# A selective-scan layer and its feed-forward block: four decay banks and two dense banks instead of three and three, other chains at both ends, another order

## The chip, the core and the metric

The kernel runs on one core of one Trainium2 chip. A core has five engines with instruction queues of their own: TensorE (PE in the profile; its weight loads are PEld), VectorE (DVE), ScalarE (ACT), GpSimd (POOL) and SyncE (SP), which here only issues transfers. They work side by side and wait for each other through semaphores. The metric is the device time of one execution in microseconds, here the median of several runs.

## What is computed

An input of 8 batches x 512 steps x 128 channels goes through a selective-scan block with 256 inner channels and 16 states, a layer norm, a feed-forward block of 384 hidden units and a second layer norm.

```python
h = x * rsqrt(mean(x * x, -1) + 1e-05) * norm_w
xs, res = split(h @ in_proj_w.T, 2)
u = silu(causal_conv(xs, conv_w, 4 taps) + conv_b)
delta, Bm, Cm = split(u @ x_proj_w.T, [64, 80])
delta = softplus(delta @ dt_proj_w.T + dt_proj_b)
state = exp(delta * A) * state + (delta * u) * Bm        # per channel, state and step
y = (sum_n state * Cm + u * D) * silu(res)
x = layernorm(x + y @ out_proj_w.T + x)
gate, up = x @ wg.T, x @ wu.T                            # weights are int32 / 127
x = layernorm(x + (silu(gate) * up) @ wd.T)
```

## The kernel before

**Layout.** One batch of 512 steps is one iteration k (`Iteration(k)`); the loop runs from k = -1 (set-up and head: only inputs are prepared) to k = 8 (the tail: only outputs are finished). In between one iteration does three things at once: it scans batch k, prepares the inputs of batch k + 1 (`it.ins`) and finishes the outputs of batch k - 1 (`it.outs`).

**The scan.** The 256 x 16 pairs of channel and state are cut into 32 groups of 128 rows (32 channels x 4 states). A group n is one step. ACT makes its decay exp(delta * A) (`exp_decay`, L573) into one of three PSUM banks, `decay_ps[n % DECAYS]`; VectorE runs the recurrence over 512 time steps in one instruction (`scan`, L964); its input is a product du * B that POOL makes for four groups at once (`multiply`, L791, 128 x 2048). Four groups are a quad. After the first scan of the next quad VectorE weighs the four states with C (`weigh`, L973), and TensorE gathers the states into `y_ps` (`sum_states`, "S" in the plan, L441 to L443: at the start of each half with a skip product u * D). C is spread into the bank `c_ps` by TensorE (`spread_c`, "C" in the plan, L432); `weigh(q)` waits for it.

**The dense work.** All other products of TensorE are jobs by name: h (transpose of the scaled input), xs0, xs1 (the convolution, four products each), res0, res1, xd, z0, z1, b0 to b3 (B spread over rows), proj, x1 (transpose), gate0 to gate2, up0 to up2, down. A job writes one of the dense banks (`BANK`), `wait_free` waits until what lay there was taken, and the taker (ACT or VectorE) frees it. delta and du are replicated over rows by transfers on SP's queue (L340).

**Order.** Nothing is scheduled by a program: `PLAN` lists what TensorE does in each of the 8 quads, `ACT_AT` and `DVE_AT` say after which of the 32 scans ACT and VectorE do each dense step, `POOL_AT` after which quad's product POOL does its small steps. On ACT step n stands behind the decay n + 1. Each engine works strictly through its list, so a step that waits holds up all behind it.

**Both ends.** In the head the weights are transposed on TensorE, the taps scaled on VectorE (L881) while POOL builds `pick0` (L744, L752), and softplus of both halves is done before the first decay. In the tail the output of the last batch goes: combination, proj, copy to r1 (L626), statistics (L1005, L984), four POOL steps (L811 to L816), normalisation on ACT (L579), x1, the gates, down, copy to y_out (L675), and the same norm again.

The names that the prediction uses: `combine` (L980), `gate` (L989), `gate_up` (L995), `take_b` (L610), `soften_first` (L912 to L941), `multiply_first` (L950).

Of the kernel before, what the change touches and what calls it, by code (L numbers as in the profile page):

```python
# [20 lines left out]
def mamba_swiglu_postln(nc, x, norm_w, in_w, conv_w, conv_b, xp_w, dt_w, dt_b, a_log, d_skip, out_w,  # L21
# [28 lines left out]
    with ctx:  # L50
# [1018 lines left out]
```

## Time and profile before

| | us |
|---|---|
| median of 3 runs (590.15 to 590.64) | 590.59 |
| the profiled execution | 589.53 |
| its span, first to last instruction | 587.8 |
| VectorE busy in it | 514.7 (88%) |
| TensorE busy | 420.6 (72%) |
| POOL busy | 418.9 (71%) |
| ACT busy | 368.8 (63%) |
| mean granted TensorE clock | 0.81 |

A row of a timeline has the start in us from the span's first instruction, the duration in us, the engine, the line, the operation, what it writes and reads, and a count where neighbours are merged; in brackets stands the idle time of the engine before it and what ended it. Neighbours on an engine overlap by some 0.08 us, so a step costs a little less than its duration. PEclk 1.00 is TensorE at 2.4 GHz, 0.50 at 1.2 GHz. A float32 product of 512 columns runs as two passes, so it counts as x2.

### The profile page before, as it was taken

Reading aid. Unit: us, or ns where it says so; the run is one execution under the profiler, and the core shown is the slowest. Engines: PE = TensorE matmul, PEld = TensorE weight load, DVE = VectorE, ACT = ScalarE, POOL = GpSimd, SP = SyncE. Lnnn points to the kernel's source line nnn. Section 1 sums busy time; section 2 is a strip of 40 time slices with the busy share of each in tenths; the row PEclk is TensorE's granted clock in tenths of the full one; section 3 lists DMA queues with packets and bytes.
Section 4 is the critical chain, followed back from the end, with each engine's and each line's share of the span. In section 5 each row is a group of like instructions: output and inputs, shape, how many; then the busy total and the mean of one; then the engine's idle time right before and its main releaser. Section 6 shows DMA issues by size and latency. Waiting matters only on the chain. (4 is left out here: it accounts for less than half of the span.)

```text
span 587.8 us, 5583 instructions
## 1 busy us (share of the span) xinstructions
PE 420.6 (72%) x1509; PEld 183.4 (31%) x1509; DVE 514.7 (88%) x552; ACT 368.8 (63%) x587; POOL 418.9 (71%) x219
## 2 busy tenths in 40 slices
PE   2977644996769766978779776977699674477653
PEld 2422111421424214422433233422442142224322
DVE  5788689988999899988999899989998899999622
ACT  2493965489557965598458956597549954553031
POOL 7559499767895789767986698577975799583111
PEclk9978856797869797897869787998879786757767
DMA  7051424600651043401460063202350065100000
GB/s 215 8 130 38 120 39 104 144 0 0 144 119 42 1 96 82 109 18 24 120 144 20 0 141 87 76 0 66 78 141 18 0 143 131 32 1 0 1 18 18
DMA packets 27366, 39.18 MB, mean 67 GB/s; under 512 B 3816, under 2 KB 10056, under 8 KB 27344
## 3 DMA queue, kind: packets, MB, share of 16 engines
q1 hardware_dynamic: 25424, 38.51, 27.6%
q10 hardware_dynamic: 1920, 0.42, 0.4%
q8 instruction: 9, 0.15, 0.1%
q14 instruction: 13, 0.11, 0.1%
HBM read 3.27 MB, written 2.10 MB: 9 GB/s over the span
## 5 line engine op out<-in xcount | busy, mean ns | idle before, releaser
L791 POOL TENSOR_TENSOR prod<-du_rep,b_rep 128x2048 f32<-128x2048 f32 x63 | 286.1, 4543 | 57.4 <-DVE state L964 49.7
L964 DVE TENSOR_TENSOR_SCAN state<-decay_ps,prod 128x512 f32<-128x512 f32 x256 | 300.3, 1208 | 22.0 <-ACT decay_ps L573 14.6
L573 ACT ACTIVATE decay_ps<-delta_rep,a_neg 128x512 f32<-128x512 f32 x252 | 170.8, 689 | 111.0 <-DVE state L964 110.5
L973 DVE TENSOR_TENSOR weighted<-state,c_ps 128x2048 f32<-128x2048 f32 x64 | 145.1, 2267 | 4.8 <-PE c_ps L432 4.2
L443 PE MATMUL y_ps<-weighted,gather 128*32 128x512 f32 x512 | 85.2, 745 | 37.7 <-DVE weighted L973 37.7
L463 PE MATMUL dense_ps<-h_t,tap_t 128*128 128x512 f32 x128 | 71.0, 706 | 0.4 <-ACT h_t L621 0.4
L432 PE MATMUL c_ps<-bc,pick 64*128 64x512 f32 x64 | 37.6, 588 | 44.8 <-DVE weighted L973 44.8
L811 POOL TENSOR_TENSOR ve<-mv,epsm 128x4 f32<-128x4 f32 x16 | 3.3, 203 | 66.5 <-DVE mv L984 66.4
L463 PEld LDWEIGHTS dense_ps<-h_t,tap_t 128*128 128x128 f32 x128 | 28.0, 230 | 48.0 <-issue 47.0
L432 PEld LDWEIGHTS c_ps<-bc,pick 64*128 64x128 f32 x64 | 13.7, 215 | 93.2 <-DVE weighted L973 60.7
L495 PE MATMUL dense_ps<-x_t,up_t 128*128 128x512 f32 x48 | 32.5, 766 | 9.2 <-DVE g_act L989 9.2
L495 PE MATMUL dense_ps<-x_t,gate_t 128*128 128x512 f32 x48 | 34.7, 812 | 4.9 <-DVE g_act L995 4.1
L500 PE MATMUL dense_ps<-down_t,g_act 128*128 128x128 f32 x192 | 37.1, 346 | 1.4 <-DVE g_act L995 1.4
L443 PEld LDWEIGHTS y_ps<-weighted,gather 128*32 128x32 f32 x512 | 10.9, 117 | 76.6 <-DVE weighted L973 45.8
L500 PEld LDWEIGHTS dense_ps<-down_t,g_act 128*128 128x128 f32 x192 | 33.4, 256 | 4.5 <-issue 4.5
L989 DVE SCALAR_TENSOR_TENSOR g_act<-g_th,dense_ps 128x512 f32<-128x512 f32 x24 | 16.4, 684 | 14.6 <-ACT g_th L666 14.6
L799 POOL TENSOR_TENSOR z_ln<-z_ln,z_pos 128x512 f32<-128x512 f32 x15 | 19.3, 1286 | 13.0 <-ACT z_ln L659 13.0
L610 ACT ACTIVATE b_rep<-dense_ps 128x512 f32<-128x512 f32 x30 | 16.1, 590 | 16.7 <-PE dense_ps L478 16.7
L456 PE MATMUL dense_ps<-ident,hx 128*128 128x128 f32 x32 | 8.3, 412 | 25.2 <-ACT hx L587 25.2
L795 POOL TENSOR_TENSOR z_wm<-z_e,z_wm 128x512 f32<-128x512 f32 x15 | 18.7, 1270 | 9.9 <-ACT z_wm L650 6.4
L483 PE MATMUL dense_ps<-out_t,g 128*128 128x128 f32 x128 | 22.6, 305 | 2.3 <-DVE g L980 2.3
L626 ACT ACTIVATE r<-dense_ps 128x512 f32<-128x512 f32 x8 | 4.8, 597 | 28.8 <-PE dense_ps L487 28.8
(130 smaller groups left out, 607.8 us busy)
## 6 DMA issues: line engine op xcount, KB each, us to landing
du_rep<-z_wm SPq DMA_DIRECT2D x64, 256.0 KB, 4.6
delta_rep<-z_ln SPq DMA_DIRECT2D x64, 256.0 KB, 4.5
out_dram<-y_out SPq DMA_DIRECT2D x8, 256.0 KB, 2.2
state<-L_attn_in_proj_w_in ACTq DMA_DIRECT2D x1, 256.0 KB, 4.1
x_all<-L_attn_x_in SPq DMA_DIRECT2D x1, 256.0 KB, 4.5
weighted<-L_ffn_w_gate_in SPq DMA_DIRECT2D x1, 192.0 KB, 10.6
weighted<-L_ffn_w_up_in SPq DMA_DIRECT2D x1, 192.0 KB, 3.3
weighted<-L_ffn_w_down_in SPq DMA_DIRECT2D x1, 192.0 KB, 4.4
```

Of the source, the lines that this page charges most:

```text
L432: mm(c_ps[:, :], pick[R:, CHUNKS + quad % CHUNKS, :], bc[it.now][R:, :], start=True, stop=True).then_inc(c_ready, 1)
L443: last = mm(y_ps[DB * c:DB * c + DB, :], gather[:, :], weighted[quad % 2][:, c, :], start=False, stop=(q == CHUNKS - 1), tile_position=(0, ...
L463: last = mm(ps[:, :], tap_t[:, n, j, :], h_t[:, j:j + T], start=(j == 0), stop=(j == TAPS - 1))
L483: mm(ps[:, i * P:(i + 1) * P], g[:, h, i * P:(i + 1) * P], out_t[:, h, :], start=(h == 0), stop=False)
L495: last = mm(ps[:, :], (gate_t if kind == "gate" else up_t)[:, n, :], x1_t[:, :], start=True, stop=True)
L500: mm(ps[:, i * P:(i + 1) * P], g_act[:, b, i * P:(i + 1) * P], down_t[:, b, :], start=(b == 0), stop=False)
L573: A(decay_ps[n % DECAYS][:, :], decay_ps[n % DECAYS][:, :] if spread_first else delta_rep[:, h, c, :], ACT.Exp, scale=a_neg[:, col:col + 1 ...
L791: TT(prod[quad % 2][:, :, :], du_rep[:, h, :, :], b, ALU.mult).then_inc(prod_ready, 1)
L795: TT(z_wm[:, h, :], z_e[:, h, :], z_wm[:, h, :], ALU.subtract).then_inc(soft_step, 1)
L799: TT(z_ln[:, h, :], z_ln[:, h, :], z_pos[:, h, :], ALU.add).then_inc(soft_step, 1)
L964: dve.tensor_tensor_scan(state[n // BLOCKS % 2][:, n % BLOCKS, :], decay_ps[n % DECAYS][:, :], prod[n // BLOCKS % 2][:, n % BLOCKS, :], 0. ...
L973: TT(weighted[quad % 2][:, :, :], state[quad % 2][:, :, :], c_ps[:, :].unsqueeze(1).broadcast_to([P, BLOCKS, T]), ALU.mult).then_inc(weigh ...
```

## The change

`DECAYS` is 4, so `DENSE` is 2: four PSUM banks for decays and two for dense jobs. `PLAN`, `BANK`, `ACT_AT`, `DVE_AT` and `POOL_AT` are new. The functions `stir` and the tables `STIR_HEAD`, `STIR_TAIL` are there, but all their counts are 0 and the plan names no such product, so nothing is issued by them.

```diff
-    DECAYS = 3
+    DECAYS = 4
     DENSE = 6 - DECAYS
@@
-                ["up1", "gate2", "up2", "C", "S", "b0", "b1"],
-                ["C", "b2", "b3", "down", "S"],
+                ["up0", "gate1", "C", "up1", "S", "gate2"],
+                ["b0", "b1", "up2", "C", "down", "b2", "b3", "S"],
@@
-        DVE_AT = {"combine": (22, 3), "stats1": 9, "gate": (20, 21, 23), "up": (21, 23, 24), "stats2": 29}
+        DVE_AT = {"combine": (18, 3), "stats1": 7, "gate": (19, 20, 23), "up": (20, 21, 25), "stats2": 29}
+        STIR_HEAD = {"h": 0, "xs0": 0, "du0": 0}
+        STIR_TAIL = {"S": 0, "x1": 0, "gate0": 0}
```

In `ACT_AT` the steps move so: y 9 to 4, h 1 to 0, silu 11 to 10, xd and x1n 13 to 15, z 15 and 16 to 16 and 17, z's exponential, z_w and z_wm 16, 17, 18 to 17, x1 16 to 17, ln 20 to 19, gates 19, 21, 24 to 18, 19, 24, b 24, 24, 29, 29 to 25, 26, 28, 28, down 29 to 27.

**TensorE around quad 4 and 5.** Here are C (L432), the gates and ups (L495), the skip product (L441) and the gathers (L443), of a middle batch. Before:

```order
L495 MATMUL dense_ps1<-x1_t,gate_t 128x512
L495 MATMUL dense_ps2<-x1_t,up_t 128x512
L495 MATMUL dense_ps0<-x1_t,gate_t 128x512
L495 MATMUL dense_ps1<-x1_t,up_t 128x512
L495 MATMUL dense_ps2<-x1_t,gate_t 128x512
L495 MATMUL dense_ps0<-x1_t,up_t 128x512
L432 MATMUL c_ps<-bc1,pick 128x512
L441 MATMUL y_ps<-u_1,skip_t 128x512
L443 MATMUL y_ps<-weighted0,gather 32x512 x4
```

After (C is L442, gates and ups L526, skip L454, gathers L456):

```order
L526 MATMUL dense_ps1<-x1_t,gate_t 128x512
L526 MATMUL dense_ps0<-x1_t,up_t 128x512
L526 MATMUL dense_ps1<-x1_t,gate_t 128x512
L442 MATMUL c_ps<-bc1,pick 128x512
L526 MATMUL dense_ps0<-x1_t,up_t 128x512
L454 MATMUL y_ps<-u_1,skip_t 128x512
L456 MATMUL y_ps<-weighted0,gather 32x512 x4
L526 MATMUL dense_ps1<-x1_t,gate_t 128x512
```

The ups and the last gate have moved behind C and behind the gathers, and gate1 and gate2 stand in one bank.

**TensorE around quad 6.** b0 to b3 are `bc,pick` (L478 before, L497 after), down is `down_t,g_act`. Before:

```order
L478 MATMUL dense_ps1<-bc0,pick 128x512
L478 MATMUL dense_ps2<-bc0,pick 128x512
L432 MATMUL c_ps<-bc1,pick 128x512
L478 MATMUL dense_ps2<-bc0,pick 128x512
L478 MATMUL dense_ps0<-bc0,pick 128x512
L500 MATMUL dense_ps1<-down_t,g_act 128x128 x3
L502 MATMUL dense_ps1<-x1,ident 128x128
```

After:

```order
L497 MATMUL dense_ps1<-bc0,pick 128x512
L497 MATMUL dense_ps0<-bc0,pick 128x512
L526 MATMUL dense_ps1<-x1_t,up_t 128x512
L442 MATMUL c_ps<-bc1,pick 128x512
L529 MATMUL dense_ps0<-x1,ident 128x128 x4
L533 MATMUL dense_ps0<-down_t,g_act 128x128 x12
L497 MATMUL dense_ps0<-bc0,pick 128x512
L497 MATMUL dense_ps1<-bc0,pick 128x512
L456 MATMUL y_ps<-weighted1,gather 32x512 x4
```

b2 and b3 have moved behind down, and up2 stands behind b0.

**TensorE at the start of a batch.** h is `ident,hx`, xs0 is `h_t,tap_t`. Before:

```order
L456 MATMUL dense_ps1<-ident,hx 128x128 x4
L432 MATMUL c_ps<-bc0,pick 128x512
L443 MATMUL y_ps<-weighted1,gather 32x512 x4
L463 MATMUL dense_ps1<-h_t,tap_t 128x512 x4
L465 MATMUL dense_ps2<-h_t,res_t 128x512
L483 MATMUL dense_ps0<-out_t,g 128x128 x2
```

After:

```order
L475 MATMUL dense_ps0<-ident,hx 128x128 x4
L482 MATMUL dense_ps1<-h_t,tap_t 128x512 x4
L456 MATMUL y_ps<-weighted1,gather 32x512 x4
L442 MATMUL c_ps<-bc0,pick 128x512
L502 MATMUL dense_ps0<-x_all,twice 128x128 x4
L506 MATMUL dense_ps0<-out_t,g 128x128 x8
```

xs0 has moved ahead of the gathers and of C; in the projection the products with x (`twice`) stand ahead of those with g.

**proj and down.** Both now add x first and then wait for g or for the last up product:

```diff
                 elif kind == "proj":
+                    for i in range(TILES):
+                        ...
+                        mm(ps[:, i * P:(i + 1) * P], twice[:, :], xk, start=(i == 0), stop=False)
                     it.wait(pe, g_ready, HALVES, -1, HALVES)
@@
                 elif kind == "down":
+                    for i in range(TILES):
+                        mm(ps[:, i * P:(i + 1) * P], ident[:, :], x1[:, i, :], start=(i == 0), stop=False)
                     it.wait_taken(pe, f"up{HID - 1}")
```

**The head.** Its jobs have an order and banks of their own; the first two products of du and B are made on VectorE from TensorE's spread du; z1's softplus and the weights of the feed-forward block move into batch 0; POOL's second select waits for the scaled taps; ACT loads the exp table ahead of xd.

```diff
-        HEAD_JOBS = ["h", "xs0", "xs1", "res0", "xd", "res1", "z0", "z1", "b1", "b0", "b2", "b3"]
+        HEAD_JOBS = ["h", "xs0", "res0", "xs1", "res1", "xd", "z0", "z1", "b0", "du0", "du1", "b1", "b2", "b3"]
@@
-                        for c in range(BLOCKS):
+                        for c in (2, 3, 0, 1):
                             replicate(du_rep, du, 0, c, du_in)
@@
+                elif kind == "du":
+                    pe.wait_ge(du_ready, 1)
+                    last = mm(ps[:, :], spread[:, n, :], du[:, 0, :], start=True, stop=True)
+                elif kind == "gate" and it.k0 == 0:
+                    pe.wait_ge(ffn_float, 3)
+                    raw = (gate_f[:, :, :], up_f[:, :, :], down_f.rearrange("p (b h) -> p b h", b=HID))[n]
+                    for b in range(HID):
+                        last = turn(ps[:, b * P:(b + 1) * P], raw[:, b, :], ident[:, :])
@@
+                silu(it, name, dst, h)
+                A(a_neg[:, 0:1], cw[:, 0, 0:1], ACT.Exp)
                 take_xd(it)
@@
+                    if it.k0 == 0:
+                        head_it = Iteration(-1)
+                        if n == 0:
+                            second_half(head_it)
+                        if n == 1:
+                            for q in (1, 2, 3):
+                                take_b(head_it, q)
+                        if n == 3:
+                            late_copy()
                     dense(it, n)
+                    if it.k0 == 0 and n == 2:
+                        second_log()
@@
             TT(x_rs[:, 0:TILES], x_ms[:, 0:TILES], powm[:, 0:TILES], ALU.pow).then_inc(rs_ready, 1)
+            pool.wait_ge(in_scaled, HALVES)
             sel(out=pick0, in_=pick0, compare_op=ALU.not_equal, fill=1.0, base=-XC,
@@
             def error(it, h):
                 it.wait(pool, wm_ready, 1, 1, 1)
                 TT(z_wm[:, h, :], z_e[:, h, :], z_wm[:, h, :], ALU.subtract).then_inc(soft_step, 1)
+                it.wait(pool, soft_step, 4, 1, 2 * h + 1)
+                TT(z_wm[:, h, :], z_wm[:, h, :], z_pos[:, h, :], ALU.add).then_inc(soft_step, 1)
```

**The tail.** In iteration 8 the copies to r1 and y_out and ACT's normalisation are left out; VectorE takes the statistics from PSUM and normalises by itself, POOL only takes the power:

```diff
+            def last_scale(ve, ve_ready, rs, rs_ready_):
+                pool.wait_ge(ve_ready, 1)
+                TT(rs[:, :], ve[:, :], powm[:, 0:TILES], ALU.pow).then_inc(rs_ready_, 1)
@@
+            def last_norm(it, name, st, step, mv, mv_ready, ve, ve_ready, rs, rs_ready_, dst, done):
+                it.wait_full(dve, name)
+                src = it.ps(name)[:, :].rearrange("p (i m) -> p i m", m=M)
+                for i in range(TILES):
+                    last = dve.bn_stats(st[:, i, :], src[:, i, :])
+                ...
+                TS(ve[:, :], mv[:, :, 1], EPS, None, ALU.add).then_inc(ve_ready, 1)
+                dve.wait_ge(rs_ready_, B)
+                for i in range(TILES):
+                    last = TS(dst[:, i, :], src[:, i, :], mv[:, i, 0:1], rs[:, i:i + 1], ALU.subtract, ALU.mult)
+                last.then_inc(done, 1)
```

## Rows read from the trace of the kernel before

**Rows 1.** Windows, first to last scan: length, busy PE, PEld, DVE, ACT, POOL, PEclk, DMA
```profile
38.66:549.51 510.85, 377.14 (x1362) 159.35 (x1360) 479.41 (x487) 340.53 (x541) 390.51 (x183) 0.81 0.29 68
```

**Rows 2.** Timeline of VectorE: start, duration (us), line, operation, idle before
```profile
166.00 1.19 DVE L964 TENSOR_TENSOR_SCAN state<-decay_ps,prod 128x512 f32<-128x512 f32 x1
...
489.60 1.19 DVE L964 TENSOR_TENSOR_SCAN state<-decay_ps,prod 128x512 f32<-128x512 f32 x1
...
496.25 0.67 DVE L980 TENSOR_TENSOR g<-y_ps,sres 128x512 f32<-128x512 f32 x1
...
497.96 2.26 DVE L973 TENSOR_TENSOR weighted<-state,c_ps 128x2048 f32<-128x2048 f32 x1
500.14 4.56 DVE L964 TENSOR_TENSOR_SCAN state<-decay_ps,prod 128x512 f32<-128x512 f32 x4
...
549.70 2.25 DVE L973 TENSOR_TENSOR weighted<-state,c_ps 128x2048 f32<-128x2048 f32 x1
```

**Rows 3.** Waits of VectorE in one batch, 230.62 to 295.24: total, times, longest
```profile
DVE state L964 <- ACT decay_ps L573: 2.3, 3, 1.6
DVE g_act L989 <- ACT g_th L666: 0.8, 1, 0.8
```

**Rows 4.** Windows, four stretches at one granted clock each (PEclk)
```profile
62.90:66.10 3.20, 3.20 (x4) 0.88 (x3) 3.20 (x2) 2.66 (x4) 0.00 (x0) 0.50 0.91 222
...
219.90:223.10 3.20, 3.20 (x14) 2.78 (x14) 3.20 (x4) 1.45 (x3) 3.12 (x3) 0.50 0.84 216
...
230.20:240.30 10.10, 7.38 (x18) 2.81 (x19) 10.10 (x13) 6.50 (x12) 9.45 (x7) 0.50 0.75 174
240.40:264.10 23.70, 20.00 (x82) 8.37 (x80) 21.52 (x24) 18.75 (x32) 14.80 (x8) 1.00 0.10 27
```

**Rows 5.** Timeline of TensorE, batch 0 and a middle batch
```profile
61.21 1.13 PE L465 MATMUL dense_ps<-h_t,res_t 128*128 128x512 f32 x2 [2.68 <-ACT u L592]
...
181.29 1.13 PE L441 MATMUL y_ps<-u,skip_t 128*128 128x512 f32 x2
...
183.35 3.70 PE L463 MATMUL dense_ps<-h_t,tap_t 128*128 128x512 f32 x8
...
200.06 1.94 PE L443 MATMUL y_ps<-weighted,gather 128*32 128x512 f32 x8 [3.18 <-DVE weighted L973]
201.93 0.79 PE L432 MATMUL c_ps<-bc,pick 64*128 64x512 f32 x1
...
204.52 1.85 PE L495 MATMUL dense_ps<-x_t,up_t 128*128 128x512 f32 x2
...
208.39 1.13 PE L495 MATMUL dense_ps<-x_t,up_t 128*128 128x512 f32 x2 [1.17 <-DVE g_act L989]
...
219.09 0.50 PE L432 MATMUL c_ps<-bc,pick 64*128 64x512 f32 x1 [2.93 <-DVE weighted L973]
...
220.32 1.65 PE L500 MATMUL dense_ps<-down_t,g_act 128*128 128x128 f32 x6
...
223.58 0.83 PE L500 MATMUL dense_ps<-down_t,g_act 128*128 128x128 f32 x6
```

**Rows 6.** Groups of the page, POOL's product
```profile
L791 POOL TENSOR_TENSOR prod<-du_rep,b_rep 128x2048 f32<-128x2048 f32 x63 | 286.1, 4543 | 57.4 <-DVE state L964 49.7
```

**Rows 7.** Head: the scalings (min, median, max ns), POOL's select, a table load
```profile
L881 DVE TENSOR_SCALAR delta_rep<-state,cw x8: 279/282/3529, 7.0 to 11.0; 128x128 f32<-128x128 f32 x8
...
8.14 3.01 POOL L752 TENSOR_SCALAR_AFFINE_SELECT delta_rep<-delta_rep 128x1024 f32<-128x1024 f32 x1
...
27.51 1.28 ACT L696 ACT_TABLE_LOAD   x1
```

**Rows 8.** Chain that ended last, three pieces of the tail: start us, us, what
```profile
559.18 0.61 ACT r L626
...
562.93 1.66 ACT x L579 x4
...
566.59 6.93 PE dense_ps L495 x10
```

More of the change, by code:

```diff
@@ new lines, in mamba_swiglu_postln @@
+        BANK = {"h": 0, "xs0": 1, "proj": 0, "xs1": 0, "res0": 1, "res1": 0, "xd": 1, "z0": 0, "z1": 1, "x1": 0,
+                "gate0": 1, "up0": 0, "gate1": 1, "up1": 0, "gate2": 1, "up2": 1, "b0": 1, "b1": 0, "down": 0,
+                "b2": 0, "b3": 1}
+        ACT_AT = {"hx": 0, "y": 4, "h": 0, "r1": 7, "silu": 10, "xd": 15, "x1n": 15, "z": (16, 17), "x1": 17,
+                  "ze": 17, "zw": 17, "zwm": 17, "ln": 19, "gate": (18, 19, 24), "b": (25, 26, 28, 28), "down": 27}
+        DVE_AT = {"combine": (18, 3), "stats1": 7, "gate": (19, 20, 23), "up": (20, 21, 25), "stats2": 29}
@@ L275, in __init__ @@
                 self.names = jobs_of(k0)
-                earlier = [n for k in range(-1, k0) for n in jobs_of(k)]
-                self.before = [sum(BANK[n] == b for n in earlier) for b in range(DENSE)]
+                earlier = [bank_of(k, n) for k in range(-1, k0) for n in jobs_of(k)]
+                self.before = [earlier.count(b) for b in range(DENSE)]
             def count(self, each, batch, n):
@@ L387, in _ @@
             pe.wait_ge(ident_ready, 1)
+            for _ in range(STIR_HEAD["h"]):
+                mm(c_ps[:, 0:P], ident[:, :], ident[:, :], start=True, stop=True)
             for h in range(HALVES):
@@ L507, in iteration @@
                     for name in it.names:
+                        if name == "h":
+                            early_weights()
                         if name == "xs0":
-                            early_weights()
+                            for _ in range(STIR_HEAD["xs0"]):
+                                stir(it, name)
                             pe.wait_ge(wt_taken, 1)
@@ L535, in iteration @@
                         if name == "C":
-                            if it.scan:
+                            if it.scan and not (it.k0 == 0 and quad == 0):
                                 spread_c(it, quad)
@@ L659, in dense @@
                     A(z_ln[:, :, :], z_e[:, :, :], ACT.Ln, bias=1.0).then_inc(ln_ready, 1)
+                if it.k0 == 0:
+                    for b in range(HID):
+                        if step == at["gate"][b]:
+                            name = f"gate{b}"
+                            it.wait_full(act, name)
+                            it.take(A((gate_t, up_t, down_t)[b][:, :, :].rearrange("p b h -> p (b h)"),
+                                      it.ps(name)[:, 0:HID * P], ACT.Copy, scale=(1.0, 1.0, SILU2)[b]), name)
                 if it.outs:
```

296 lines of the change are left out of this document (163 added, 133 removed).

## The prediction

> **What bounds the kernel now.** I read the stretches first. Between the first scan and the last, 38.66 to 549.51 us, VectorE is busy 479.41 of 510.85 us [rows 1]; ahead of it lie 38.7 us of set-up, behind it 38.3 us of tail. Then I read VectorE's own timeline, to see how far it is from its own pace. Batch 7, which prepares no successor, never waits: its first scan starts at 489.60 and its last weighing (L973) at 549.70, so 60.1 us is what a batch costs VectorE alone. The batches before it take (489.60 - 166.00) / 5 = 64.7 us [rows 2]. So 4.6 us a batch are waits. The waits of one batch name ACT's decays (2.3 us) and the tanh (0.8) [rows 3]; the remainder is the overlap lost around them. What could be won in the middle is thus 6 batches x 4.6 = 28 us, no more.
>
> Last I read TensorE. It has two speeds: it is granted 1.00 in 240.4 to 264.1 us and 0.50 (1.2 instead of 2.4 GHz) in 230.2 to 240.3 [rows 4]. It fell after it had idled 3.18 us (the eight gathers from 200.06 took 1.94), 2.93 us (the stretch from 219.9 to 223.1) and, in batch 0, 2.68 us, where it was at 0.50 from 62.9 us; it did not fall after 1.17 us [rows 4, 5]. Once low it stayed so for 3.2 to 10 us, while it worked nearly without a pause. At 0.50 two passes of a 512-column product take 1.85 us instead of 1.13, or 1.0 in a stream; the next value of C 0.79 instead of 0.50; three down products of 128 columns 1.65 instead of 0.83 [rows 5].
>
> **The change, part by part.** *Four decay banks.* ACT may run four scans ahead instead of three, one scan (1.12 us, 4.48 for four [rows 2]) more. That covers the longest ACT wait before, 1.6 us, only together with the moved steps, and ACT's own work does not shrink: in steps 15 to 19 it now has xd, x1, both z, three 1,024-wide steps and the logarithm in a row. I take these ACT waits as gone, -2.3 us, which is part of the 4.6 and is not counted twice: I build the new batch from 60.1 up.
>
> *Two dense banks and the new order.* Nothing is added or removed on VectorE. What counts is each place where VectorE now meets a chain over TensorE.
>
> Place 1, the third gate. From the end of quad 4's weighing VectorE has three products (0.67 less 0.08 of overlap) and three scans until it wants tanh(gate2): 3 x 0.59 + 3 x 1.12 = 5.1 us. In that time TensorE must do C, up1, the skip product with four gathers, and gate2, one behind the other since the bank of gate2 is that of gate1: 0.50 + 1.13 + 2.06 (181.29 to 183.35) + 1.13, and ACT a tanh of 0.59: 5.4 us less the overlaps, so no slack at full clock. At half clock it is 0.79 + 1.85 + 3.9 + 1.85 + 0.59 = 9.0, 3.9 us late [rows 2, 5]. Before, all gates and ups stood ahead of C. Just before this place TensorE waits for the weighing: gate1 ends about 2.2 us ahead of it. I take a fall, and a climb back halfway: 2.0 us late; ends 0 and 3.9.
>
> Place 2, the down projection. b2 and b3 now stand behind it. From the last up product (step 25) to the next batch's first scan VectorE has six scans, one weighing and the statistics: 6.7 + 2.2 + 1.0 = 9.9 us. The chain in that time: twelve down products (4 x 0.68), the copy 0.6, b2 and b3 on TensorE and, behind a decay, on ACT (0.8 + 1.3), and POOL's product of 4.54 [rows 6]: 9.9. Again no slack, and the decay of step 29 waits behind the copy too. TensorE has 3 us of idle in the 4.7 ahead of it (tanh, b0's copy, the weighing). At half clock each group of three costs 1.44 instead of 0.68 before its neighbour starts: 3.0 us late in all. I take 1.9; ends 0 and 3.0. Before, b2 and b3 stood ahead of down, and POOL's product did not wait for it.
>
> Place 3, the batch's start. xs0 now stands ahead of the gathers and C. VectorE wants the gathers 1.12 + 2.18 + 3 x 1.12 = 6.7 us after its first scan starts. TensorE starts xs0 about 0.6 to 1.1 after it (it waits for hx, a transpose and the copy of h, some 2 to 3 us with little work in it): 3.70 + 1.1 makes 5.4 to 5.9, in time; at half clock 0.6 + 7.3 + 1.9 = 9.8, 3.1 late [rows 5]. I take 1.5.
>
> Place 4, z1. ACT needs it in step 17, ahead of three steps of 1 us each and the decay of step 19. TensorE idles 2.35 us until xd is copied, then does z0, C, the gathers and z1, 3.4 us, with 1 us to spare; at half clock 6.2, so 1.8 late. I take 0.8. Place 5, gate0 behind x1's copy: ends 0 and 1.9, I take 0.3, since place 4 has spread the work.
>
> The sum is 2.0 + 1.9 + 1.5 + 0.8 + 0.3 = 6.5, a batch of 66.6 us, 1.9 above the present one: 6 batches make +11.4. Batch 7 has places 1 and 5 and an idler TensorE, against nothing before: I take +3.0 (ends 0 and 5).
>
> The idle stretches that the new order leaves are 2.0 to 2.7 us (2.7 between x1 and the gathers of quad 3), between the row of 1.17 that kept the clock and that of 2.68 that lost it, and often two lie close together; they are nearer to 2.68, so I price them as falls.
>
> The Trainium skill (TensorE: Matmul & The Clock Gate, Why this matters for your kernels) advises to leave no idle gaps of more than about 3 us between bursts. By that rule no gap of the new order would cost the clock. The rows above hold two falls after less, 2.93 and 2.68 us, so the rule is not safe here; what it would make is the first rival.
>
> *The head.* POOL's second select on pick0 now waits for VectorE's scaling of the taps. Before, one of the eight scalings took 3.53 us instead of 0.28, beside that select of 3.01 [rows 7]; free of it they are done 3.2 earlier. The res products stand between xs0, xs1 and xd: +1.9 less overlap, and the transposes ahead of h: together +2.0. An exp table load of 1.28 [rows 7] goes under the xd products, an addition of 0.7 leaves the chain behind the logarithm, z1's part (three steps of 0.65 and two loads, 4.5 us) moves behind the first decays, and the first two products come from TensorE instead of a DMA, but VectorE waits for them: -1.3, -0.7, -4.5 and +1.7. The first scan moves from 38.7 to about 32.7. But the moved part stands again between decays 1 and 4: scan 4 gains about 2.3 us, and POOL's products, two of which VectorE waits for in batch 0, leave 2.0 at its end. I take -2.0; ends -6 and +1.
>
> *The tail.* Gone: the copy of r1 (0.61), that of y_out (0.6), two short POOL steps each time (about 0.4), part of each ACT normalisation (1.66 against four VectorE instructions of about 0.28) [rows 8], the x products behind g and behind the last up product (1.3 and 0.9). Added: gate2 and up2 share a bank, so the FFN piece of 6.93 plus its activations becomes about 1.6 longer. Sum -4.2; ends -6 and 0, the worse if TensorE stays low throughout.
>
> Total: 11.4 + 3.0 - 2.0 - 4.2 = +8.2 on the profiled execution's 589.5 us: 597.7. The median of the runs is 1.1 above that execution: 598.8, so 599 us.
>
> **Rivals.** *Full clock in spite of the gaps.* If gaps under 2.7 us cost nothing, every place above has its slack of about zero and a batch takes 60.3 us: 6 x -4.4 - 2.0 - 4.2 = -32.6, so 558 us. For it: the row of 1.17, and that TensorE stays at 1.00 for 23.7 us in the middle of each batch. Against: 2.68 and 2.93.
>
> *Falls at half of the places.* Faster, with one mechanism: the clock falls only after the longest gap, between x1 and the gathers, and ahead of place 1, and is back before down. It decides at place 2: while POOL's product is in time the batch keeps 1.9 us, and place 3 another 1.3. A batch of 63.4: 6 x -1.3 + 2.0 - 2.0 - 4.2 = -12, so 579 us. For it: in the present batches the low stretches end after 3.2 to 7 us in two cases of three.
>
> *An exchange.* The waits add up to the old 4.6 and only the ends differ: 6 x 0 + 2 - 6.2 = -4, to 0 with a poorer tail: 587 to 591.
>
> *Worse.* TensorE stays at 0.50 through most of the batch, since it never works long enough at a stretch: stalls of 8.4, a batch of 68.5: 6 x 3.8 + 4 - 6 = +21, 611 us.
>
> **The numbers.** The forecast has a chance of 0.48 (its own range 592 to 606), worse 0.09, exchange 0.12, half of the places 0.19, full clock 0.12. A measurement of this kernel tells about 0.2%, 1.2 us, from no change. Faster takes full clock, half and most of the exchange: 0.37; same 0.06; slower 0.57. The range runs from 570, which leaves full clock out, to 609.
>
> **What would show it.** Right: first scans of batches 66 to 67 us apart; VectorE waiting in each batch about 2 us for the tanh of gate2, about 2 us for POOL's first product and 1 to 2 us ahead of the combination in step 3 for TensorE's gathers; hardly any wait for decays outside step 19; the eight scalings done by 8.7 us; the first scan near 33 us; a tail of about 34 us. Wrong: a granted clock of 1.00 through the batch, a spacing under 62, or scans waiting mainly for ACT, which would mean that the fourth bank and not TensorE decides.

## The result, and the profile after

The changed kernel is slower: 599.85 us in the median (598.34 to 603.11, 4 runs) against 590.62 for the kernel before (590.15 to 591.46, 4 runs), a ratio of 1.016 with a 95% interval of 1.012 to 1.021. The forecast was 599, with a range of its own from 592 to 606. The profiled execution took 603.11 us (span 601.4), the longest of the four, so sizes read from it are some 3 us too large in sum; most of these may sit in the head (see the last section).

| stretch (us, from the profiles) | before | after | difference | forecast |
|---|---|---|---|---|
| start to first scan | 38.66 | 37.15 | -1.5 | -6.0 |
| batch 0 | 62.95 | 66.75 | +3.8 | +4.0 |
| batches 1 to 6, each | 64.67 | 66.71 | +2.04 (x6: +12.3) | +1.9 (+11.4) |
| batch 7, first to last scan | 58.71 | 61.96 | +3.25 | +3.0 |
| last scan to end | 39.44 | 35.24 | -4.2 | -4.2 |
| span | 587.8 | 601.4 | +13.6 | +8.2 |

(The forecast put -2.0 on the first two rows together: 6.0 won ahead of the first scan, 4.0 lost again in batch 0.)

From the start of the first scan to the end of the last, as in [rows 1]: length, busy PE, PEld, DVE, ACT, POOL, PEclk, DMA.

```profile
37.15:567.33 530.18, 399.63 (x1376) 163.37 (x1374) 479.95 (x489) 347.45 (x549) 390.97 (x184) 0.80 0.28 66
```

VectorE is busy as long as before (479.95 against 479.41), in 19.3 us more. So all of the loss between the scans is idle time of VectorE. Its waits over batches 1 to 6, with the one ahead of batch 7's first scan (total, times, longest):

```profile
DVE g_act L1079 <- ACT g_th L720: 13.2, 16, 2.2
DVE state L1038 <- ACT decay_ps L620: 8.8, 9, 1.5
DVE state L1038 <- POOL prod L864: 7.6, 6, 1.4
DVE g L1054 <- PE y_ps L456: 4.4, 3, 1.8
DVE g_act L1085 <- PE dense_ps L526: 0.6, 2, 0.4
```

These are 34.6 us, 5.8 a batch, against 3.6 before by the same count. Of the 3.6, [rows 3] has 2.3 for decays and 0.8 for the tanh; the same view has a third wait, for C ahead of a weighing, which the prediction took for lost overlap:

```profile
DVE weighted L973 <- PE c_ps L432: 0.5, 1, 0.5
```

Here is batch 5 on VectorE (371.09 to 438.14, 67.05 us), the instructions that wait and the next first scan; in brackets the idle time and who ended it:

```profile
371.09 1.22 DVE L1038 TENSOR_TENSOR_SCAN state<-decay_ps,prod 128x512 f32<-128x512 f32 x1 [1.21 <-POOL prod L864]
...
408.61 0.69 DVE L1079 SCALAR_TENSOR_TENSOR g_act<-g_th,dense_ps 128x512 f32<-128x512 f32 x1 [1.02 <-ACT g_th L720]
...
419.73 0.69 DVE L1079 SCALAR_TENSOR_TENSOR g_act<-g_th,dense_ps 128x512 f32<-128x512 f32 x1 [1.31 <-ACT g_th L720]
...
432.43 1.22 DVE L1038 TENSOR_TENSOR_SCAN state<-decay_ps,prod 128x512 f32<-128x512 f32 x1 [1.45 <-ACT decay_ps L620]
...
438.14 1.23 DVE L1038 TENSOR_TENSOR_SCAN state<-decay_ps,prod 128x512 f32<-128x512 f32 x1 [1.21 <-POOL prod L864]
```

The first and the last row are POOL's first product, for this batch and for the next; between them stand gate0, gate2, and the decay of step 29 behind the copy of y_out. These are places 5, 1 and 2 of the prediction. TensorE in the same batch, at the places where its clock fell:

```profile
396.10 0.95 PE L493 MATMUL dense_ps<-xd,dt_t 64*128 64x512 f32 x1 [2.41 <-ACT xd L652]
...
403.28 1.94 PE L456 MATMUL y_ps<-weighted,gather 128*32 128x512 f32 x8 [1.85 <-DVE weighted L1047]
...
405.87 2.07 PE L526 MATMUL dense_ps<-x_t,gate_t 128*128 128x512 f32 x2
...
412.74 0.50 PE L442 MATMUL c_ps<-bc,pick 64*128 64x512 f32 x1 [1.96 <-DVE weighted L1047]
413.33 2.02 PE L526 MATMUL dense_ps<-x_t,up_t 128*128 128x512 f32 x2
...
423.79 0.79 PE L442 MATMUL c_ps<-bc,pick 64*128 64x512 f32 x1 [1.00 <-DVE weighted L1047]
```

And the granted clock (the last number but two) of those stretches:

```profile
396.50:399.50 3.00, 3.00 (x11) 0.48 (x9) 3.00 (x4) 2.95 (x8) 2.83 (x2) 0.50 0.00 0
403.50:410.50 7.00, 7.00 (x15) 1.96 (x7) 5.67 (x7) 5.29 (x8) 6.06 (x5) 0.54 0.00 0
413.50:416.50 3.00, 3.00 (x4) 0.95 (x4) 2.81 (x4) 2.96 (x5) 3.00 (x1) 0.50 0.72 117
424.00:431.00 7.00, 7.00 (x33) 6.55 (x33) 6.98 (x6) 0.00 (x0) 0.40 (x1) 0.54 0.12 34
```

So the clock falls four times between z0 and down, behind idle stretches of 2.41, 1.85, 1.96 and 1.00 us (with another of 1.41 shortly ahead of the last one). Each of them is shorter than the stretches of 2.68 to 3.18 us behind which it fell in [rows 4, 5]. The length of one stretch does not decide: in [rows 5] the clock stood through 1.17 us.

### The profile page after: what moved, and what is told of

Read it like the earlier page. It is cut to its first block, busy times and chain, and to the rows that moved or that the text cites. A ratio compares the mean times of both kernels' runs of the same rounds, so it can differ in the third digit from the quotient of the medians.

```text
span 601.4 us, 5630 instructions
## 1 busy us (share of the span) xinstructions
PE 442.3 (74%) x1513; PEld 185.9 (31%) x1513; DVE 513.7 (85%) x562; ACT 366.8 (61%) x581; POOL 417.3 (69%) x214
## 4 chain that ended last, share of the span: by engine, by line
PE 35%; DVE 26%; issue 16%; ACT 11%; POOL 7%; DMA 1%; SPq 1%; DVEq 0%; ACTq 0%; POOLq 0%
DVE weighted L1047 14%; DVE state L1038 9%; PE dense_ps L482 8%; PE dense_ps L526 5%; PE y_ps L456 5%; ACT decay_ps L620 5%; POOL prod L864 4%; PE dense_ps L533 3%; PE y_ps L454 2%; PE dense_ps L493 2%; PE c_ps L442 2%; PE dense_ps L529 2%; PE dense_ps L484 2%; SPq L358 1%; DVE g_act L1085 1%
## 5 line engine op out<-in xcount | busy, mean ns | idle before, releaser
L620 ACT ACTIVATE decay_ps<-delta_rep,a_neg 128x512 f32<-128x512 f32 x252 | 165.4, 684 | 61.0 <-DVE state L1038 60.9
L456 PE MATMUL y_ps<-weighted,gather 128*32 128x512 f32 x512 | 89.1, 777 | 25.6 <-DVE weighted L1047 25.6
L442 PE MATMUL c_ps<-bc,pick 64*128 64x512 f32 x64 | 39.6, 618 | 39.0 <-DVE weighted L1047 38.9
L442 PEld LDWEIGHTS c_ps<-bc,pick 64*128 64x128 f32 x64 | 14.4, 225 | 97.5 <-DVE weighted L1047 64.1
L526 PE MATMUL dense_ps<-x_t,gate_t 128*128 128x512 f32 x48 | 35.9, 838 | 5.8 <-ACT x_t L703 4.0
L526 PE MATMUL dense_ps<-x_t,up_t 128*128 128x512 f32 x48 | 34.5, 809 | 6.1 <-DVE g_act L1079 2.8
L720 ACT ACTIVATE g_th<-dense_ps 128x512 f32<-128x512 f32 x24 | 14.3, 597 | 39.4 <-PE dense_ps L526 39.4
L493 PE MATMUL dense_ps<-xd,dt_t 64*128 64x512 f32 x32 | 25.3, 887 | 16.9 <-ACT xd L652 16.9
L729 ACT ACTIVATE y_out<-dense_ps 128x512 f32<-128x512 f32 x7 | 4.2, 597 | 49.4 <-PE dense_ps L533 49.4
L456 PEld LDWEIGHTS y_ps<-weighted,gather 128*32 128x32 f32 x512 | 11.1, 119 | 66.4 <-issue 34.6
L454 PE MATMUL y_ps<-u,skip_t 128*128 128x512 f32 x32 | 23.5, 826 | 10.2 <-DVE weighted L1047 10.2
L533 PE MATMUL dense_ps<-down_t,g_act 128*128 128x128 f32 x192 | 30.6, 332 | 0.0
L533 PEld LDWEIGHTS dense_ps<-down_t,g_act 128*128 128x128 f32 x192 | 30.5, 252 | 0.1
L497 PE MATMUL dense_ps<-bc,pick 64*128 64x512 f32 x32 | 12.2, 457 | 15.6 <-DVE g_act L1079 8.5
L875 POOL TENSOR_TENSOR z_ln<-z_ln,z_wm 128x512 f32<-128x512 f32 x15 | 19.1, 1275 | 6.1 <-ACT z_ln L706 6.1
```

The costliest lines, as they stand in the source:

```text
L442: mm(c_ps[:, :], pick[R:, CHUNKS + quad % CHUNKS, :], bc[it.now][R:, :], start=True, stop=True).then_inc(c_ready, 1)
L454: mm(y_ps[:, :], skip_t[:, h, :], u[side][:, h, :], start=True, stop=False)
L456: last = mm(y_ps[DB * c:DB * c + DB, :], gather[:, :], weighted[quad % 2][:, c, :], start=False, stop=(q == CHUNKS - 1), tile_position=(0, ...
L493: last = mm(ps[:, :], dt_t[:, n, :], xd[0:R, :], start=True, stop=True)
L526: last = mm(ps[:, :], (gate_t if kind == "gate" else up_t)[:, n, :], x1_t[:, :], start=True, stop=True)
L533: last = mm(ps[:, i * P:(i + 1) * P], g_act[:, b, i * P:(i + 1) * P], down_t[:, b, :], start=False, stop=(b == HID - 1 and i == TILES - 1))
```

## Experiments

All are timed in five rounds against the kernel before on the same chip; the changed kernel's own ratio is 1.016 (1.012 to 1.021).

**e1, idle products on TensorE.** Each writes 256 columns into the bank of the job that it stands ahead of. The count behind a name stands for repeated entries.

```diff
-["h", "xs0", "S", "C", "proj"]
+["~h" x5, "h", "~xs0" x2, "xs0", "S", "C", "proj"]
-["z0", "C", "S", "z1"], ["x1", "S", "C", "gate0"]
+["~z0" x7, "z0", "C", "S", "z1"], ["~x1" x3, "x1", "~gate0" x2, "S", "C", "~gate0" x2, "gate0"]
-["up0", "gate1", ...], ["b0", ..., "down", "b2", "b3", "S"]
+["up0", "~gate1" x3, "gate1", ...], ["~b0" x3, "b0", ..., "down", "~b2" x2, "b2", "b3", "S"]
```

> The changed kernel with 29 idle products of 256 columns a batch on TensorE, put where it waits (ahead of h 5, xs0 2, z0 7, x1 3, gate0 4, gate1 3, b0 3, b2 2); nothing else changed. Theory A, the half clock makes the waits: the granted clock of the batches rises from about 0.80 to above 0.95, the waits for tanh(gate2) (1.1 us a batch), for POOL's first product (1.05), at the combination (0.7) and for the decay of step 19 (0.9) mostly go, a batch falls from 66.7 to 61 to 63 us, and the whole to 565 to 578 us (ratio to the kernel before 0.955 to 0.98). Theory B, the chains are too long even at full clock, or the idle products take as much as they give: a batch stays at 66 to 68 us, 598 to 608 us, ratio 1.01 to 1.03.

Measured: 579.38 us, ratio 0.982 (0.980 to 0.985). Batches 1 to 6, clock and VectorE's waits:

```profile
105.93:482.71 376.78, 332.94 (x1452) 170.13 (x1450) 364.20 (x386) 273.53 (x432) 301.49 (x147) 0.99 0.31 71
```
```profile
DVE state L1038 <- POOL prod L864: 7.5, 7, 1.4
DVE g L1054 <- PE y_ps L456: 1.9, 1, 1.9
DVE g_act L1079 <- ACT g_th L720: 1.2, 6, 0.2
DVE state L1038 <- ACT decay_ps L620: 0.9, 1, 0.9
```

The clock is at 0.99, a batch takes 62.8 us (62.3 from batch 2 on), and 20 us of the changed kernel's time are gone. The waits for the tanh, for decays and at the combination were the half clock. The one for POOL's first product was not: it stays at 1.1 to 1.4 us at full clock. Theory A holds, with a total just above its range, since batch 0 took 69.1 us instead of 66.8: idle products ahead of h held decay 3 back there.

**e2, gate2 ahead of the skip product and the gathers (place 1).**

```diff
-["up0", "gate1", "C", "up1", "S", "gate2"],
+["up0", "gate1", "C", "up1", "gate2", "S"],
```

> The changed kernel with gate2 ahead of the skip product and the four gathers in quad 5 (place 1 of the prediction undone in part). If place 1 is the chain C, up1, skip, gathers, gate2: the wait for the third tanh (1.1 us a batch in the mean, 1.8 in batch 7) goes, and 4 to 8 us of the whole with it, 592 to 596 us, ratio 1.003 to 1.009. Rival: what is won there is lost at the next chain (up2, down, POOL's first product), since gate2 early only moves the slack: 598 to 601 us, ratio 1.013 to 1.018.

Measured: 587.94 us, ratio 0.994 (0.992 to 0.996), 11.9 us below the changed kernel and more than either theory gave. The wait for gate2's tanh is gone in all batches; a batch falls by 2.2 us to 64.5, though that wait was only 1.1. The rest came behind it: up2, down and b2 follow sooner, and the waits for POOL's product go from 7.6 us to 2.8, those for decays from 8.8 to 5.8:

```profile
DVE state L1038 <- ACT decay_ps L620: 5.8, 6, 1.5
DVE g L1054 <- PE y_ps L456: 5.5, 4, 1.7
DVE state L1038 <- POOL prod L864: 2.8, 3, 1.4
```

Places 1 and 2 were one chain, not two. The granted clock of the six batches was 0.83, against 0.81 in the changed kernel, so most of this gain is the order's. If the clock is worth what it was in e1 (3.9 us a batch for 0.18), the 0.02 are some 0.4 us of the 2.2, an estimate; the two are not taken apart.

**e3 and e10, the last gathers ahead of xs0 (place 3), in e10 C as well.**

```diff
-["h", "xs0", "S", "C", "proj"],
+["h", "S", "xs0", "C", "proj"],      # e3
+["h", "S", "C", "xs0", "proj"],      # e10
```

> The changed kernel with the last gathers of a batch ahead of xs0 (place 3 undone). If place 3 is as predicted: the wait of the combination in step 3 (0.7 us a batch in the mean, in three batches of six) goes, nothing else moves, since xs0 is wanted only in step 10: minus 4 to 5 us, 595 to 596 us, ratio 1.008 to 1.010. Rival: TensorE now has to wait for the weighing right behind h, idles there and falls to half clock; xs0, xd and z come later and the decay of step 19 waits more: no gain or a loss, 599 to 605 us, ratio 1.015 to 1.025.

> The changed kernel with the last gathers of a batch and C ahead of xs0 (in e3 only the gathers were; C then came late behind xs0, and the weighing of step 4 waited 2.6 us a batch for it). If place 3 is right: the waits of the combination in step 3 (0.7 us a batch) and of e3's weighing are both gone, nothing else grows by more than 0.3: 594 to 597 us, ratio 1.005 to 1.011. Rival, TensorE's idle ahead of the gathers and its falls only move: xs0 later, the other waits grow by as much: 598 to 602 us, ratio 1.012 to 1.020.

Measured: e3 609.20 us, 1.032 (1.030 to 1.034); e10 605.10 us, 1.026 (1.023 to 1.028), both above both theories. The combination's wait went in both, and a larger one came. In e3 it is the weighing of step 4, which waits for C behind xs0 (15.6 us in six batches). In e10 it is the decay of step 12 (2.0 us a batch): xs0 begins later, proj stands behind it, and ACT's copy of r1 and its silu stand ahead of that decay. TensorE's rows, then ACT's:

```profile
307.91 1.93 PE L456 MATMUL y_ps<-weighted,gather 128*32 128x512 f32 x8 [3.34 <-DVE weighted L1047]
309.77 0.79 PE L442 MATMUL c_ps<-bc,pick 64*128 64x512 f32 x1
310.50 5.27 PE L482 MATMUL dense_ps<-h_t,tap_t 128*128 128x512 f32 x8
```
```profile
318.48 0.60 ACT L673 ACTIVATE r<-dense_ps 128x512 f32<-128x512 f32 x1 [4.70 <-PE dense_ps L506]
```

Place 3 of the new order, 0.7 us a batch, was the cheapest of the three. My expectation of e3 overlooked C.

**e4 and e5, b2 and b3 ahead of down (place 2), without and with idle products.** e5 is e4 with the idle products of e1.

```diff
-["b0", "b1", "up2", "C", "down", "b2", "b3", "S"],
+["b0", "b1", "up2", "C", "b2", "b3", "down", "S"],
-"b": (25, 26, 28, 28), "down": 27}
+"b": (25, 26, 27, 27), "down": 28}
```

> The changed kernel with b2 and b3 ahead of the down projection on TensorE, their copies on ACT after scan 27 and the copy of y_out after scan 28 (place 2 undone). If place 2 is the chain down, y_out copy, b2, b3, POOL's product: the wait for POOL's first product (1.05 us a batch) and that for the decay of step 29 (0.55) go, minus 1.6 x 7 = 11 us at most, less a new wait for the y_out copy ahead of the statistics in step 29 of up to 1 us a batch: 589 to 597 us, ratio 0.998 to 1.010. Rival, an exchange: down 1 to 2 us later makes the statistics and with them all of steps 29 to 31 wait as long as POOL's product did: 599 to 603 us, ratio 1.013 to 1.022.

> The changed kernel with the idle products of e1, and b2 and b3 ahead of the down projection as in e4. In e1, at full clock, VectorE still waited 1.1 to 1.4 us a batch for POOL's first product. Theory A: that is the length of the chain down, y_out copy, b2, b3, product (place 2), and at full clock down has the slack to stand last: the wait goes, no new one of more than 0.3 us comes ahead of the statistics of step 29, a batch falls from 62.2 to about 61.1, 571 to 574 us, ratio 0.967 to 0.972. Theory B, an exchange as in e4 (a wait of 0.9 us ahead of the statistics and more at the combination): 577 to 581 us, ratio 0.977 to 0.984.

Measured: e4 602.09 us, 1.019 (1.016 to 1.021), an exchange as the rival said: POOL's product is in time, and VectorE waits for y_out (5.5 us in six batches) and at the combination (11.4) instead. e5: 570.49 us, 0.965 (0.963 to 0.967), theory A and half a us below its range. The clock is 1.00 throughout, VectorE's waits in the six batches are 4.1 us, and from batch 2 on a batch takes 60.8 us, 0.7 above what VectorE needs alone:

```profile
104.56:472.39 367.83, 331.70 (x1452) 170.29 (x1450) 363.03 (x385) 272.94 (x432) 303.18 (x147) 1.00 0.32 73
```
```profile
DVE g L1054 <- PE y_ps L456: 1.9, 1, 1.9
DVE g_act L1079 <- ACT g_th L720: 1.2, 6, 0.2
DVE state L1038 <- ACT decay_ps L620: 1.0, 1, 1.0
```

One edit is worth nothing at half clock and 8.9 us at full clock (e5 against e1; in the profiles 1.5 us a batch): only there is down behind b2 and b3 early enough for the statistics.

**e6 and e9, does the old order want the clock too?** e6 puts idle products of the same kind into the kernel before, ahead of h, of the gathers in quad 3 and of C in quad 6; e9 only those ahead of h.

```diff
-["h", "C", "S", "xs0", "res0", "proj"]
+["~h" x8, "h", "C", "S", ...]                       # e6 and e9
+["z1", "~gate0" x7, "S", "C", "gate0", ...]         # e6
+["~b2" x6, "C", "b2", "b3", "down", "S"]            # e6
```

> The kernel before with 21 idle products of 256 columns a batch on TensorE in its three long waits (ahead of h 8, ahead of the gathers of quad 3 7, ahead of C in quad 6 6). Theory A, it is the new order that needs the full clock: the old one is bound by VectorE's waits for ACT's decays (2.3 us a batch), which no clock of TensorE takes away; the granted clock rises above 0.9, but a batch stays between 63.8 and 64.8 and the whole at 583 to 591 us, ratio 0.988 to 1.001. Theory B, the half clock costs the old order as much as the new one (e1 won 3.9 us a batch): a batch of 61 to 62.5, 563 to 575 us, ratio 0.953 to 0.975.

> The kernel before with 8 idle products of 256 columns a batch, ahead of h alone, where TensorE idles 4.4 us and nothing that is wanted stands behind them (in e6 those ahead of the gathers and of C themselves waited for a copy of ACT and held the gathers back, so e6 tells nothing of the clock). Theory A, the old order has slack where TensorE is slow: the granted clock rises from 0.81 to 0.85 or more, the half-clock stretch of 10 us behind h goes, the wait ahead of the weighing in step 8 (0.5 us a batch) with it, nothing else; a batch 64.2, the whole 586.5 to 590.5 us, ratio 0.993 to 1.000. Theory B, the clock is worth as much here as in the new order: more than 1.5 us a batch, below 581 us, ratio under 0.984.

Measured: e6 624.50 us, 1.058 (1.056 to 1.060), outside both theories. The idle products ahead of the gathers want a bank that is free only once ACT has copied x1, so TensorE first waits 3.54 us and then does most of them at half clock, with the gathers behind:

```profile
277.41 5.40 PE L449 MATMUL dense_ps<-x_all,ident 128*128 128x256 f32 x14 [3.54 <-ACT x_t L662]
282.74 1.06 PE L443 MATMUL y_ps<-weighted,gather 128*32 128x512 f32 x8
```

e9: 593.51 us, 1.007 (1.005 to 1.008), slower than theory A (590.5 at most). The stretch 230 to 240, at 0.50 in [rows 4], is at 1.00, and a batch takes 64.7 us as before: VectorE's waits for decays grow from 2.3 to 2.6 as that for the tanh shrinks to 0.4. The ends are longer instead (batch 0 +1.3, the tail +1.4). At that stretch, then, the old order gains nothing from the clock. For the other low stretches it stays open, as e6 did not test it.

**e7, POOL's second select behind the scalings, in the kernel before.**

```diff
             TT(x_rs[:, 0:TILES], x_ms[:, 0:TILES], powm[:, 0:TILES], ALU.pow).then_inc(rs_ready, 1)
+            pool.wait_ge(in_scaled, HALVES)
```

> The kernel before with one edit of the head: POOL's second select on pick0 waits for the eight scalings of the taps. Theory A: the scaling of 3.53 us takes 0.28, the transposes of the taps end 2 to 3 us earlier, the convolution starts at about 13.0 instead of 14.8, but it then runs its first five passes at 1.2 GHz (1.06 us each instead of 0.59), as in the changed kernel: the first scan moves by 0 to 0.6 us, 590 us, ratio 0.998 to 1.001. Theory B: the 1.8 us come through to the first scan (36.9 instead of 38.7): 588.8 us, ratio 0.996 to 0.998.

Measured: 586.50 us, 0.992 (0.990 to 0.994), better than both theories. The eight scalings take 1.66 us together, where before one alone took 3.53 [rows 7], the first products on the taps start at 11.80 instead of 14.84, and the first scan at 35.74 instead of 38.66:

```profile
6.94 1.66 DVE L882 TENSOR_SCALAR delta_rep<-state,cw 128x128 f32<-128x128 f32 x8
```
```profile
11.80 7.32 PE L463 MATMUL dense_ps<-h_t,tap_t 128*128 128x512 f32 x16
```

The slow first passes that I expected did not come (one of 16).

**e8, another order in batch 0.** The logarithm of z1 stands behind decay 6 here. e12 has the same order, with the logarithm behind decay 5.

```diff
+                        if name == "b1":
+                            spread_delta(3)
@@
-                if it.k0 == 0:
-                    spread_delta(3)
@@
-        H_FIRST = 1
+        H_FIRST = 2
@@
-                            for q in (1, 2, 3):
-                                take_b(head_it, q)
+                            take_b(head_it, 1)
+                        if n == 2:
+                            for q in (2, 3):
+                                take_b(head_it, q)
@@
-                    if it.k0 == 0 and n == 2:
+                    if it.k0 == 0 and n == 5:
                         second_log()
```

> The changed kernel with another order at the start of batch 0: TensorE's fourth spread delta ahead of b2 and b3; on ACT the copies of b2, b3 and of h behind decay 3 instead of ahead of it, the logarithm of z1 with its two table loads behind decay 6 instead of decay 3. Theory A, the two waits of 2.7 and 2.4 us ahead of scans 3 and 4 are ACT's list alone: scan 3 starts at about 43 instead of 45.4, scan 4 at 46 to 47 instead of 49.4 (POOL's product, 45.9, is next), batch 0 falls from 66.8 to about 64 and the whole by 2.5 to 3.5 us, ratio 1.010 to 1.013. Theory B: batch 0 is bound later by ACT's silu in step 10 and by the transfer of du's second half in step 16, and gives it back: 599 to 600 us, ratio 1.014 to 1.018.

Measured: 601.16 us, 1.018 (1.015 to 1.020), no gain: theory B. Scans 3 and 4 do not wait any more (5.1 us), scan 12 waits 0.7 instead of 3.0 us, and scan 16 waits 5.15 instead of 0.44 us: POOL's product needs du's second half, which is as late as before. In addition VectorE's first step of z1's softplus, 0.40 us in the changed kernel, now meets POOL's product:

```profile
41.59 2.19 DVE L1027 TENSOR_SCALAR z_wm<-z_e 128x512 f32<-128x512 f32 x1
43.70 1.21 DVE L1040 TENSOR_TENSOR_SCAN state<-decay_ps,prod 128x512 f32<-128x512 f32 x1
...
70.51 1.22 DVE L1040 TENSOR_TENSOR_SCAN state<-decay_ps,prod 128x512 f32<-128x512 f32 x1 [5.15 <-POOL prod L866]
```
```profile
38.97 4.53 POOL L866 TENSOR_TENSOR prod<-du_rep,b_rep 128x2048 f32<-128x2048 f32 x1 [1.68 <-DMA du_rep<-z_wm]
```

**e11 and e12, the fastest version.** e11 is e5 with idle products at both ends and none in quad 0 of batch 0; e12 adds e8's order, and POOL makes du's second half ahead of the product of quad 2:

```diff
-        STIR_HEAD = {"h": 0, "xs0": 0, "du0": 0}
-        STIR_TAIL = {"S": 0, "x1": 0, "gate0": 0}
+        STIR_HEAD = {"h": 22, "xs0": 3, "du0": 7}
+        STIR_TAIL = {"S": 14, "x1": 12, "gate0": 4}
@@ e12
                             error(Iteration(-1), 1)
-                        if it.k0 == 0 and quad == 2:
                             soften(Iteration(-1), 1)
                             scale_u(Iteration(-1), 1)
```

> e5 (idle products, b2 and b3 ahead of down) with idle products also in the head (22 small ones ahead of the first transposes, 3 ahead of xs0, 7 ahead of the first spread delta) and in the tail (14 ahead of the last gathers, 12 ahead of x1, 4 ahead of gate0), and none in quad 0 of batch 0, where e5 waited 4.8 us instead of 2.7 ahead of scan 3. Theory A: first scan at 33.5 to 34.5 in every execution, batch 0 at 66.8 instead of 69.8, a tail 1 to 2 us shorter: 563.5 to 566.5 us, ratio 0.953 to 0.958. Theory B, the head and the tail have other limits and batch 0 gives its gain back in step 16: 568 to 571 us, ratio 0.961 to 0.966.

> e11 with the order of batch 0 changed as in e8 (the fourth spread delta ahead of b2 and b3, the copies of b2, b3 and h behind decay 3, the logarithm of z1 behind decay 5), and POOL's last two steps of z1's softplus and du ahead of the product of quad 2 instead of behind it. In e8 scans 3 and 4 no longer waited (5.1 us less), and scan 16 waited 5.1 us more, since POOL makes du's second half, and its transfer starts, no earlier. Theory A, that was the whole cause: du leaves 4.5 us earlier, scan 16 waits under 2 us, batch 0 is 3 to 5 us shorter than in e11: 559.5 to 563 us, ratio 0.947 to 0.953. Theory B, scan 8 then waits 3 us for the product of quad 2, and decays with ACT's silu bound the rest of batch 0: within 1.5 us of e11.

Measured: e11 568.49 us, 0.960 (0.955 to 0.964); e12 562.91 us, 0.954 (0.951 to 0.956), both faster than either given kernel. By its median e11 is in theory B's range, 2 us below e5; its runs stand in two groups, 561 to 563 and 568.5 us. e12 is theory A. Batch 0 is 67.0 us in e11 and 62.9 in e12, where scan 16 no longer waits and scan 8 waits 3.4; the tail is 0.8 to 1.0 us shorter than e5's. The head got worse: the 7 idle products are 14 passes, at half clock in e12 and for the first 3.3 us in e11, and end 2.7 us after delta is ready in e11 and 4.1 in e12, so the first scan comes at 36.3 and 37.0 us instead of e5's 34.7. From e12:

```profile
27.95 6.04 PE L559 MATMUL decay_ps<-x_all,ident 128*128 128x256 f32 x14
33.82 1.02 PE L437 MATMUL decay_ps<-z_ln,spread 128*128 128x512 f32 x2
```

e12 without these 7 was not tried.

## Why the prediction was right

**The middle.** The step was: 60.1 us for VectorE alone plus five places, 66.6 a batch; measured 66.7. The places, from VectorE's timeline, mean of batches 1 to 6:

| | forecast | measured |
|---|---|---|
| 1, tanh of gate2 | 2.0 | 1.1 (1.3 to 2.2 in four batches, 0 in two) |
| 2, POOL's first product, decay of step 29 | 1.9 | 1.27 + 0.55 |
| 3, combination in step 3 | 1.5 | 0.74 (1.3 to 1.8 in three batches) |
| 4, decay of step 19 | 0.8 | 0.9 |
| 5, gate0, and behind it gate1 and up1 | 0.3 | 0.9 + 0.3 |
| overlap lost | 0 | 0.9 |

The mechanism is shown: with the clock at 0.99, places 1 and 4 and the wait for gate0 are gone and place 3 stays in one batch of six (e1), and a batch loses 3.9 us. But 1 and 3 were priced too high, and place 5 was too small, 0.3 against 1.2: gate0 stands behind x1's copy and behind the gathers at half clock (1.94 us, then 2.07 for the product). The sum came out because these errors and the lost overlap, which had no term, cancel: 6.5 against 6.6. That is luck in the number, not in the mechanism. The step "ACT's waits are gone" held: outside steps 19 and 29 no decay is waited for, and the 1.6 us ahead of scan 15 have disappeared. No run has the fourth bank without the new order, so which of the two removed them is not shown.

Batch 7 has places 1 and 5, as forecast: VectorE waits 1.8 us for gate2's tanh and 0.9 for gate0's, where it did not wait before, which makes 2.7 of the +3.25 (forecast 3.0).

Place 2 was a chain of 9.9 against 9.9, and this was half the truth. At full clock it is still 1.1 to 1.4 us late (e1), so the forecast's first rival, 60.3 a batch at full clock, was too fast; 62.3 is what this order gives there, and 60.8 needs b2 and b3 ahead of down (e5).

**The falls.** I priced gaps of 2.0 to 2.7 us as falls. The rows above have falls after 1.85, 1.96 and 2.41 us, so they were. The Trainium skill (TensorE: Matmul & The Clock Gate, Why this matters for your kernels) advises to leave no idle gap of more than about 3 us. By it none of these would cost anything, and the trace says otherwise; keeping below 3 us did not protect this kernel.

**The head is what failed.** Two steps of it. First, "the first scan moves from 38.7 to about 32.7": it came at 37.15, and in the eight kernels with this head between 34.4 and 37.2 (see the last section), so even the earliest is 1.7 us late. The taps are scaled in time (1.66 us for eight, done at 8.8), but the transposes ahead of h, priced at part of 2.0, let the convolution start at 13.0, against 11.80 in e7 with the old order. It then ran five passes at 1.06 us instead of 0.59, and the spread of delta and du at half clock:

```profile
13.00 5.89 PE L482 MATMUL dense_ps<-h_t,tap_t 128*128 128x512 f32 x8 [0.89 <-DVE dt_t L976]
...
32.57 2.04 PE L437 MATMUL decay_ps<-z_ln,spread 128*128 128x512 f32 x2 [2.11 <-DVE z_ln L1010]
34.40 1.91 PE L517 MATMUL dense_ps<-z_wm,spread 128*128 128x512 f32 x2
```

Second, "scan 4 gains about 2.3 us": it lost 2.1 (49.37 instead of 47.24), though the first scan was 1.5 earlier. ACT has the copies of b2, b3 and h and then the logarithm with two table loads between its decays:

```profile
42.20 1.08 ACT L657 ACTIVATE b_rep<-dense_ps 128x512 f32<-128x512 f32 x2 [1.14 <-PE dense_ps L497]
44.15 0.69 ACT L668 ACTIVATE h_t<-dense_ps,nw 128x512 f32<-128x512 f32 x1 [0.87 <-PE dense_ps L475]
44.74 0.65 ACT L620 ACTIVATE decay_ps<-decay_ps,a_neg 128x512 f32<-128x512 f32 x1
45.41 1.28 ACT L764 ACT_TABLE_LOAD   x1
46.70 0.63 ACT L764 ACTIVATE z_ln<-z_e 128x512 f32<-128x512 f32 x1
47.35 1.28 ACT L620 ACT_TABLE_LOAD   x1
48.65 0.69 ACT L620 ACTIVATE decay_ps<-delta_rep,a_neg 128x512 f32<-128x512 f32 x1
```

I had counted the work moved behind decay 1 as filling ACT's idle time. Further on in batch 0, scan 12 waits 3.0 us, and 0.8 and 1.3 us go ahead of scans 20 and 21. In exchange scans 16 and 24, which waited 2.7 and 2.0 us for POOL's product before, wait 0.4 and 0.5. By e8 ACT's list is not the last limit either: even with it out of the way, scan 16 waits for du.

**The tail.** -4.2 was forecast and -4.2 came. Statistics and normalisation on VectorE answer to the ACT pieces of [rows 8]:

```profile
575.69 0.89 DVE L1066 BATCH_NORM_STATS2 st<-dense_ps 128x6 f32<-128x128 f32 x4 [3.17 <-PE dense_ps L506]
...
578.32 1.37 DVE L1074 TENSOR_SCALAR x<-dense_ps,mv,rs 128x128 f32<-128x128 f32 x4 [1.12 <-POOL rs L885]
```

No experiment took the tail by itself; that each of its terms was right is argued, not shown. The terms as the prediction lists them add up to about 3.7 (with 0.54 for each normalisation, 1.66 less four times 0.28), not to 4.2, so a part of the agreement is luck.

## What to carry to other kernels

An order whose chains have no slack at full clock should be timed with TensorE kept busy and without: this order was worth -1.8% with idle products and +1.6% without, and moving b2 ahead of down gave 1.5% only once the clock held. Idle products must need nothing that is later than the wait they fill, or they become the wait (e6, and the head of e11). A wait can be worth more than its own length if the chain behind it also has no slack: gate2's 1.1 us a batch gave back 2.2.

## What the runs showed of the hardware that was not expected

- A VectorE instruction with a scalar operand that starts beside a GpSimd instruction can last until that one has ended. The scaling of 0.28 us took 3.53 [rows 7], and 0.28 once POOL's select waited for it (e7); z_wm's step of 0.40 us took 2.19 in e8 and 3.07 in e12, each ending 0.3 to 0.6 us behind POOL's instruction. The one wait on POOL is worth 0.8% of the kernel before. The Trainium skill (SBUF — State Buffer, Who interferes with whom) says that a `tensor_scalar` can enter a mode that uses the port pair shared with GpSimd, and that whichever of the two issues first then blocks the other for the whole instruction. These three pairs agree. Not every pair does: in the kernel before, five scalings that started beside POOL's step on x_rs (7.16 to 8.30) took 0.28 us each.
- The head's first products vary where the program does not. Eight kernels have the same head up to the first spread of delta (the changed one, e1 to e5, e8, e10): of xs0's eight passes 5, 5, 5, 0, 4, 0, 0 and 4 took 0.85 to 1.19 instead of 0.59 us, and their first scans came between 34.4 and 37.2 us. That can be most of the 3 us by which the profiled execution was above the median, and what splits e11's runs into 561 to 563 and 568.5 us; neither was shown.
- TensorE's clock fell behind idle stretches of 1.85 and 1.96 us, and once behind two short ones of 1.41 and 1.00 us, while in [rows 5] it stood through one of 1.17.
